# Expert down projections as seven block products (Strassen's scheme) on one Trainium2 core, and the tie step of the routing on GpSimd

## What is computed

```python
def _golden_weights(x, Wr, temperature):
    inh = jax.nn.sigmoid(x @ Wr / temperature)
    in_zone = (inh >= GOLDEN_LOWER) & (inh <= GOLDEN_UPPER)
    distance = jnp.abs(inh - GOLDEN_CENTER)
    weights = jnp.exp(-distance / 0.1) * in_zone.astype(x.dtype)
    ...
    fb = jnp.exp(-distance / 0.3)
    _, top2 = jax.lax.top_k(fb, 2)
    ...
gate = jnp.einsum('btd,edf->betf', x, Wg)
up = jnp.einsum('btd,edf->betf', x, Wu)
h = jax.nn.silu(gate) * up
e_out = jnp.einsum('betf,efd->betd', h, Wd)
out = jnp.einsum('bte,betd->btd', weights, e_out)
```

## Time and profile before

| what | value |
|---|---|
| median of three runs | 3265.81 us |
| time of the profiled execution | 3272.1 us |
| its span, first to last instruction | 3270.3 us |
| mean granted TensorE clock | 0.997 |
| TensorE busy, whole span | 3229.4 us (99%) |
| VectorE, ScalarE, GpSimd busy | 74%, 65%, 61% |
| last layer, in the span | from about 2640 us to the end |

### The profile page before, as it was taken

One profiled execution on the slowest core, in us unless ns is written; L12 is line 12 of the kernel. 1 busy time (PEld: TensorE's weight loads), 2 busy tenths in 40 slices (PEclk: granted clock), 3 DMA queues, 4 the chain that ended last, 5 costly groups with the idle time before them and its releaser, 6 DMA issues.

```text
span 3270.3 us, 106843 instructions
## 1 busy us (share of the span) xinstructions
PE 3229.4 (99%) x35420; PEld 2536.6 (78%) x35420; DVE 2423.5 (74%) x7665; ACT 2123.1 (65%) x6385; POOL 1988.8 (61%) x3965
## 2 busy tenths in 40 slices
PE   9999999999999999999999999999999999999999
PEld 7888888888766786777777777777776678888888
DVE  5677777777788767887888888788877866555555
ACT  5777777777756556777777777777775533333333
POOL 4666666666666446777777777777765662222232
PEclk9999999999999999999999999999999999999999
DMA  3111111111212242111111111111125640000000
GB/s 101 55 55 55 55 54 54 54 55 55 74 46 73 69 127 61 46 46 46 44 50 45 47 45 47 44 47 50 45 62 138 178 129 14 13 13 13 13 13 14
DMA packets 275878, 183.64 MB, mean 56 GB/s; under 512 B 116797, under 2 KB 272661, under 8 KB 275749
## 3 DMA queue, kind: packets, MB, share of 16 engines
q1 hardware_dynamic: 271109, 177.36, 19.3%
q10 hardware_dynamic: 4640, 4.59, 0.5%
HBM read 141.41 MB, written 36.21 MB: 54 GB/s over the span
## 4 chain that ended last, share of the span: by engine, by line
PE 59%; DVE 1%; DMA 1%; issue 0%; ACT 0%; SPq 0%; DVEq 0%; ACTq 0%
PE bank_e L3083 12%; PE c_ps_a L1134 7%; PE b_ps_a L1100 7%; PE bank_e L3096 7%; PE s_ps_a L1107 5%; PE out_ps_a L1160 3%; PE a_ps_a L1111 3%; PE c_ps_a L1111 2%; PE b_ps_a L1111 2%; PE out_ps_a L1144 2%; PE c_ps_a L1193 2%; PE m_ps_r L2538 2%; PE c_ps_a L1172 1%; PE out_ps_a L1232 1%; PE c_ps_a L1183 1%; PE m_ps_r L2576 1%
## 5 line engine op out<-in xcount | busy, mean ns | idle before, releaser
L1264 ACT ACTIVATE probs_a<-s_ps_a,neg_max_a 128x257 f32<-128x257 f32 x1024 | 474.4, 476 | 82.9 <-DVE neg_max_a L1384 78.1
L1318 POOL TENSOR_SCALAR probs_a<-probs_a,gated_a 128x256 f32<-128x256 f32 x1024 | 473.6, 483 | 26.5 <-POOL gated_a L1327 26.3
L1384 DVE TENSOR_REDUCE neg_max_a<-s_ps_a 128x1 f32<-128x257 f32 x1024 | 424.0, 414 | 0.0
L3039 POOL TENSOR_TENSOR hidden_e<-gate_p,own_p 128x256 f32<-128x256 f32 x192 | 139.2, 730 | 414.1 <-ACT gate_p L3197 413.9
L574 POOL TENSOR_SCALAR probs_i<-probs_i,inv_sum_i 128x256 f32<-128x256 f32 x510 | 243.9, 492 | 133.7 <-DVE inv_sum_i L738 129.3
L1383 DVE TENSOR_TENSOR self_s_a<-s_ps_a,mask_a 128x32 f32<-128x32 f32 x1024 | 185.8, 181 | 135.0 <-PE s_ps_a L1107 134.9
L553 ACT ACTIVATE probs_i<-s_ps_i,neg_max_i 128x257 f32<-128x257 f32 x512 | 236.3, 474 | 58.7 <-DVE neg_max_i L812 57.0
L392 PE MATMUL a_ps_i<-w_k_i,ctx_t_i 128*128 128x256 f32 x1024 | 253.7, 391 | 0.0
L1134 PE MATMUL c_ps_a<-w_v_a,ctx_t_a 128*32 128x256 f32 x4096 | 247.6, 382 | 0.0
L379 PE MATMUL c_ps_i<-w_v_i,ctx_t_i 128*128 128x256 f32 x1024 | 247.5, 379 | 0.0
L1100 PE MATMUL b_ps_a<-ctx_t_a,w_qk_a 128*128 128x256 f32 x1016 | 241.3, 380 | 0.0
(11 more groups left out here) (430 smaller groups left out, 8712.5 us busy)
## 6 DMA issues: line engine op xcount, KB each, us to landing
ctx_t_i<-in_ctx_t SPq DMA_DIRECT2D x128, 256.0 KB, 2.7
ctx_t_a<-in_ctx_t SPq DMA_DIRECT2D x128, 256.0 KB, 2.7
mask_a<-in_L_xattn_mask SPq DMA_DIRECT2D x512, 4.0 KB, 1.5
v_bd_a<-v_self_a SPq DMA_DIRECT2D x512, 8.0 KB, 1.8
x_tok_i<-in_x SPq DMA_DIRECT2D x32, 128.0 KB, 2.0
x_res_i<-in_x SPq DMA_DIRECT2D x32, 128.0 KB, 2.4
x_after<-y_tok_i SPq DMA_DIRECT2D x32, 128.0 KB, 1.8
x_tok_d<-x_after SPq DMA_DIRECT2D x32, 128.0 KB, 2.3
```

The source lines that it names most:

```text
L1264: act.activation(probs[:, t, :], s_ps[:, g, 0:K], ACT.Exp, bias=neg_max[:, t:t + 1], accum_out=row_sum[:, t:t + 1]).then_inc(exp_done, 1)
L1318: pool.tensor_scalar(probs[:, t, 0:2 * P], probs[:, t, 0:2 * P], gated[:, t:t + 1], 1.0, ALU.mult, ALU.mult).then_inc(probs_ready, 1)
L1384: dve.tensor_reduce(neg_max[:, 4 * f + g:4 * f + g + 1], s_ps[:, g, 0:K], AX.X, ALU.max, negate=True).then_inc(max_ready, 1)
```

## The change

**Down projection.** The eight calls of 256 columns per expert become seven block products of two calls with 128 columns each (`down`). The rows are the stationary operand, the weights the moving one. They are spread over the expert after: `down_3` of the expert two before stands behind P1, `down_1` behind 7a, `down_7` behind P6, `down_6` behind 7b, and `down_2`, `down_4`, `down_5` between P5 and P3. The very last expert keeps the ordinary form (`whole_down`).

**Sums of rows.** GpSimd forms four sums of blocks of `hidden` per expert (`sum_hidden`), right behind the last hidden quarter, at the start of the next expert.

**Sums of weights.** VectorE forms four block sums of the down weights per expert, in turn 0 alone (`sum_down`).

**Results.** ScalarE makes four more copies out of PSUM per expert (`down_copy`, `down_last`), VectorE three more additions (`down_join`), and the result stands in SBUF, in `y`. `take` reads `y`, no longer PSUM, and comes two experts later instead of one: behind `hide_last`, ahead of the join `own11` (in experts 0 and 2 around the joins).

**Banks.** `second` and `seventh` have one bank each instead of two, and the transposed tokens two banks instead of four.

**Routing.** The multiplication and the addition of `route_ties` move to GpSimd (`route_pairs`, in expert 1). On VectorE `route_zone` moves to the start of expert 0, `route_ranks` to the start of expert 1, and the rest, from the reduction to `route_weights`, to the start of expert 2, all ahead of the join `own11`. On ScalarE, silu of `own11` now stands ahead of the second copy of the chain (except in expert 0).

`moments` goes from expert 3 to expert 4; `normalize` stays at the end of expert 5.

```diff
@@ PE
         def expert(i, e, begins, ends):
...
             product(into, w_block(e, 0, 0), x_block(0, 0), chain_full, True)
+            if e > 1 or not begins:
+                down_3(i, e - 2)
...
+            pe.wait_ge(joined, joined_count(i, e - 1, 21))
+            product(seventh_ps, w_block(e, 1, 0), x_sum[3][:, :], seventh_full, True)
...
+            if downs:
+                down_1(i, e - 1)
+            pe.wait_ge(joined, joined_count(i, e - 1, 11))
+            product(second_ps, w_block(e, 0, 1), x_block(1, 0), second_full, True)
...
+            if downs:
+                down_7(i, e - 1)
             pe.wait_ge(copied, copy_count(i, e, 7))
...
-            if e or not begins:
-                down(i, e - 1, 0)
+            if downs:
+                down_6(i, e - 1)
...
             pe.wait_ge(copied, copy_count(i, e, 6))
             product(into, w_sum[1][:, e, :, :], x_sum[1][:, :], chain_full)
...
-            if e or not begins:
-                down(i, e - 1, 1)
+            if downs:
+                down_2(i, e - 1)
+                down_4(i, e - 1)
+                down_5(i, e - 1)
+        def down(into, rows, weights, start=False):
             for t in range(2):
+                last = pe.matmul(into[:, t * P:t * P + P], rows[:, t * P:t * P + P], weights, start=start and t == 0, stop=True, skip_group_check=True)
             last.then_inc(down_full, 1)
@@ GpSimd
+        def sum_hidden(i, e):
+            pool.wait_ge(hidden12_ready, count(i, e))
...
+            pool.tensor_tensor(hidden_sum[3][:, :], hidden_block(e, 11), hidden_block(e, 12), ALU.subtract).then_inc(down_sums, 1)
+            pool.tensor_tensor(hidden_sum[1][:, :], hidden_block(e, 12), hidden_block(e, 22), ALU.add).then_inc(down_sums, 1)
...
+            pool.tensor_tensor(hidden_sum[2][:, :], hidden_sum[1][:, :], hidden_block(e, 11), ALU.subtract).then_inc(down_sums, 1)
...
+            pool.tensor_tensor(hidden_sum[4][:, :], hidden_block(e, 21), hidden_sum[2][:, :], ALU.subtract).then_inc(down_sums, 1)
@@ VectorE
                 if e == 0:
                     route_logits(i)
+                    route_zone(i)
                 if e == 1:
+                    route_ranks(i)
+                if e == 2:
                     route_ties(i)
+                    route_fallback(i)
+                    route_totals(i)
+                    route_weights(i)
+                if takes and e not in (0, 2):
+                    take(i, e - 2, 1)
+                    take(i, e - 2, 0)
                 dve.wait_ge(second_full, count(i, e))
                 dve.wait_ge(copied, copy_count(i, e, 1))
+                join(i, e, 11, second_ps, parts.first)
...
                 if follows:
+                    down_joins(i, e - 1)
+                if begins:
+                    sum_down(e)
+                if e == 4 and not ends:
                     moments(dve, i + 1)
@@ take
-                last = dve.scalar_tensor_tensor(out=acc[n][:, t, :], in0=down_ps[n][:, t * D:t * D + D], scalar=weight[:, 2 * n + t, e % E:e % E + 1], in1=before_sum, op0=ALU.mult, op1=ALU.add)
+                last = dve.scalar_tensor_tensor(out=acc[n][:, t, :], in0=y[n][:, t, :], scalar=weight[:, 2 * n + t, e % E:e % E + 1], in1=before_sum, op0=ALU.mult, op1=ALU.add)
@@ ScalarE
+                else:
+                    silu(i, e, 11)
                 act.wait_ge(joined, joined_count(i, e - 1, 21))
                 act.wait_ge(chain_full, count(i, e, 4, 2))
                 copy(parts.second, chain[e % 2])
```

More of the change, by code:

```diff
@@ L3041, in turn @@
         def turn(i, begins, ends):
             for e in range(E):
-                if begins and e + 1 < E:
-                    sum_weights(e + 1)
+                if e or not begins:
+                    sum_hidden(i, e - 1)
+                if e == 0 and not begins:
+                    keep_last(i)
+                if begins and e == 0:
+                    sum_weights(1)
+                if begins and e + 2 < E:
+                    sum_weights(e + 2)
                 hide(i, e, 11)
+                if e == 1:
+                    route_pairs(i)
@@ new lines, in down_7, with down_6, down_2 @@
+        def down_7(i, e):
+            pe.wait_ge(down_sums, sum_count(i, e, 3))
+            pe.wait_ge(down_joined, down_joined_count(i, e - 1, 21))
+            down(down_seventh, hidden_sum[3], down_sum[3][:, e % E, :], True)
+        def down_6(i, e):
+            pe.wait_ge(down_sums, sum_count(i, e, 2))
+            pe.wait_ge(down_copied, down_copy_count(i, e, 1))
+            down(down_chain[e % 2], hidden_sum[2], down_sum[2][:, e % E, :])
+        def down_2(i, e):
+            wait_hidden(pe, i, e, 21)
+            pe.wait_ge(down_joined, down_joined_count(i, e - 1, 11))
+            down(down_second, hidden_block(e, 21), down_block(e % E, 1, 0), True)
@@ L3118, in expert @@
         def expert(i, e, begins, ends):
-            into, second, seventh = chain[e % 2], second_ps[e % 2], seventh_ps[e % 2]
+            into = chain[e % 2]
+            downs = e > 0 or not begins
             if begins:
@@ L3161, in turn, with whole_down @@
                 expert(i, e, begins, ends)
+        def whole_down(into, n, lanes, done):
+            for t in lanes:
+                at, col = (2 * n + t) * P, (t - lanes[0]) * D
+                for k in range(TILES):
+                    last = pe.matmul(into[:, col:col + D], hidden[(E - 1) % 2][:, k, at:at + P], w_down[:, E - 1, k, :], start=k == 0, stop=k == TILES - 1)
+            last.then_inc(done, 1)
         pe.wait_ge(*before.high)
@@ L3381, in turn @@
                 join(i, e, 22, chain[e % 2], parts.seventh)
-                if e == 1:
-                    route_totals(i)
-                    route_weights(i)
-                    take(i, 0, 0)
+                if takes and e in (0, 2):
+                    take(i, e - 2, 0)
                 if follows:
-                    take(i, e - 1, 1)
-                if e == 0:
-                    route_ranks(i)
-                if e == 3 and not ends:
+                    down_joins(i, e - 1)
+                if begins:
+                    sum_down(e)
+                if e == 4 and not ends:
                     moments(dve, i + 1)
@@ L3399, in vector @@
         hide_last(LAST, E - 1)
-        take(LAST, E - 1, 0)
+        take(LAST, E - 2, 1)
+        take(LAST, E - 2, 0)
         finish()
```

300 lines of the change are left out of this document (187 added, 113 removed).

## The result

The changed kernel takes 3288.53 us (median of four runs, 3285.45 to 3290.94), against 3267.82 us for the kernel before on the same chip: ratio 1.0064, 95% interval 1.0046 to 1.0081. It is slower by 0.64%, 20.7 us between the medians. Between the two profiled executions the spans differ by 3287.5 - 3270.3 = 17.2 us.

The account below looks back on a forecast made before the run. TensorE bounds the layer, busy 78.00 of 78.00 us a turn. Walking the engines in order gave six loop turns +16, turn 0 +6, turn 7 +1.3, start +0.4: together +24 on 3265.8, so 3290 us; range 3264 to 3310.

Parts of the forecast that it names:

- TensorE's own work, -22 us: Down products: 28 records at 0.111 us replace 16 taking 3.46 us; 9.15 us an expert, 0.35 less, over 63 experts.
- Rival C: Short down records don't hold 0.111 us: at 0.125 a record +37 us, 3303; at 0.137 +52, 3318; chance 0.15.
- the change doesn't do what it says: Down products: an eighth fewer columns but no TensorE time saved, the case from 0.124 us a record on.
- VectorE and GpSimd block each other, 0.88 us a pair: Expert start: takes reading two SBUF tensors alternate with GpSimd's sums, 0.88 us a pair against 0.34 to 0.40 alone.
- Rival A: Takes are not held by GpSimd but routing instructions are: a turn 78.1 us, +6 us, 3272; chance 0.14.
- rival B: Blocking costs nothing because GpSimd, idle half the time, starts later: 75.3 us a turn, -17 us, 3249; chance 0.16.
- It goes both ways: GpSimd's instructions beside VectorE's are held too: its sums near 0.9 us, where a product alone takes 0.72.
- The way to P5: Late join `own11` delays silu, then ScalarE's second copy, opening TensorE holes of 1 to 2 us ahead of P5.
- Experts 1 and 2, 1.8 and 1.45 us: TensorE waits ahead of P5, as routing pieces ahead of join `own11` delay it: 1.8 us in expert 1, 1.45 in 2.
- Expert 5, 1.4 us: TensorE waits 1.4 us ahead of P5: `moments` delays `hide_last` and GpSimd's power holds the first take until 3.2.
- Turn 0, +6 us: GpSimd's gate and up sums and VectorE's 32 down sums hold each other up ahead of `down_7` and `down_6`: +6 us.
- The tie step at zero: Moving the tie step to GpSimd in expert 1 costs nothing, as GpSimd waits for silu 21 there anyway.

Follow-up runs that it names:

- narrow_sums: The change, with GpSimd's four sums per expert forming only 8 of 256 columns and four down products reading plain hidden blocks: 3254.6 us, ratio to before 0.9957.
- takes_behind: The change, with all takes behind the joins, n=1 behind `own11` and n=0 behind `own22`, as in experts 0 and 2: 3296.8 us, ratio to before 1.0083.
- copy_first: The change, with ScalarE's second copy of the chain ahead of silu 11 in experts 1 to 7, the earlier order: 3268.7 us, ratio to before 1.0000.
- grouped_late: `three_moved` with turn 0's 32 down sums made 12 and GpSimd's weight sums behind each expert's last product: 3263.2 us, ratio to before 0.9984.
- three_moved: The change, with second copy ahead of silu 11, `route_ranks` behind join `own11`, GpSimd's fourth sum behind `hide` 11: 3261.9 us, ratio to before 0.9981.

## Why the prediction was right, and where it was off

It said 3290 us with the sign slower, and 3288.5 came out. Point by point:

- **TensorE's own work, -22 us: right.** 9.17 us for an expert without a hole (9.15 forecast); down records 0.11 us apart. Rival C and "the change doesn't do what it says" fall with that.
- **VectorE and GpSimd block each other, 0.88 us a pair: right.** `narrow_sums` shows it by itself: takes from 942 to 479 ns and 34 us off the time, with VectorE's code unchanged; and `takes_behind` shows 478 ns with nothing left out. The rule of the Trainium skill (SBUF — State Buffer, Who interferes with whom) is borne out for the takes. Rival A falls with the median of 942, rival B with the loop turns, which came out 1.6 us longer, not shorter. What B would have been can be seen: without the blocking 3254.6, where it said 3249.
- **It goes both ways: only in part.** "GpSimd's sums near 0.9" holds for the second sum (median 902 ns); the other three have 746, 788 and 732 (727, 732 and 729 in `takes_behind`, away from the takes). VectorE pays for most of it.
- **The way to P5: right.** `copy_first` cuts it and takes back 20 us of the 20.7 between the medians, 17.3 of the 18.8 between the last layers.
- **Experts 1 and 2, 1.8 and 1.45 us: right,** 1.98 and 1.39 lost.
- **Expert 5, 1.4 us: wrong, the largest mis-sized term of a loop turn.** The step that failed is "GpSimd's power of 1.02 us holds the first take until 3.2". The timelines of expert 5, GpSimd's and VectorE's:

```profile
2936.74 1.02 POOL L3026 TENSOR_TENSOR inv_std_e<-var_eps_e,half_e 128x4 f32<-128x4 f32 x1 [1.87 <-DVE var_eps_e L3366]
2937.73 0.75 POOL L3075 TENSOR_TENSOR hidden_sum_p<-hidden_e 128x256 f32<-128x256 f32 x1
```

```profile
2937.01 2.61 DVE L3492 SCALAR_TENSOR_TENSOR acc_e<-y_p,weight_e,acc_e 128x256 f32<-128x256 f32 x4
```

  The first two takes begin during the power, 0.27 and 0.67 us into it, and last 477 ns each; the four take 2.61 us, less than the 3.08 of an expert without a power. A long GpSimd instruction with four columns to read doesn't hold VectorE. Expert 5 loses 0.44 us and expert 6 0.14 (0.3 forecast). With this step alone mended the walk gives 79.2 us a turn instead of 80.2; measured 79.5. Six turns were sized at +16 and measured +9.5.
- **Expert 0, 0.5 us: too large.** From P3 to P3 it takes 10.05 us in the loop, and 9.94 in `narrow_sums`: about 0.1 lost.
- **Experts 3, 4 and 7 without a hole: nearly.** Expert 3 loses 0.29 us ahead of `down_3`, which waits for the down joins, and in expert 2 takes stand ahead of these. It is no matter of the blocking: in `narrow_sums` expert 3 takes 9.46 us as well.
- **Turn 0, +6 us: too small.** It was 8.3. The holes ahead of `down_7` that it named are there (1.17 and 0.54 us in experts 5 and 6). But the longest one, 3.25 us, stands ahead of P5 in expert 2 and not ahead of `down_7` or `down_6`, and behind it the clock costs 1.6 us that it lacked: expert 2 takes 14.33 us from P3 to P3, 5.2 more than an expert without a hole. It named the 32 small sums without a price of their own; without them turn 0 is 6.6 us shorter.
- **Start and end:** +0.4 forecast, -1.6 measured, in a stretch of the program that varies by 7 us over kernels with the same code, mostly with the granted clock. Turn 7: +1.3 forecast, +1.0 measured.
- **The tie step at zero: wrong by its size.** It saves some 5 us; the walk had its effect inside the 2.7 us a turn, but the text didn't tell it as a gain.

So the total was hit a little by compensation: the loop was sized 6.5 us too long and turn 0 2.3 us too short. The rest is between the measures: the medians lie 20.7 us apart, the profiled spans 17.2, and the last layers 18.8. Against the +24 of the sum that is 3 to 7 us too much; that the time itself was missed by 1.5 us only is luck in part, since the median of the kernel before came out 2.0 us higher (3267.8) than the one that the sum started from. Why the clock fell in some executions and not in others, ahead of the last layer and in turn 0, stays open.

## What to carry to other kernels

Before moving work to the engine with the most idle time, look at what its neighbour does in the same microsecond: here a VectorE instruction of 128x256 with two SBUF inputs took 0.94 us instead of 0.48 beside GpSimd's sums of the same size, and sums of busy time don't show it. Then follow the late result to where the bounding engine waits, queue by queue: the cheapest mend here was one line of order on a third engine, ScalarE, worth 20 of the 20.7 us. And count the instructions that meet a busy neighbour, the small ones too (128x32 took 0.72 us instead of 0.18); wide ones are no way out while the neighbour is busy (`grouped_late`). What can stand later (the fourth sum) should.

## What was unexpected of the hardware

- GpSimd's power of 128x4 (1.02 us) doesn't hold VectorE, while its 128x256 sums of 0.72 us do: takes of 475 to 479 ns begin inside the power in all six loop turns, against a median of 942 beside the sums. By the rule of the Trainium skill (SBUF — State Buffer, Who interferes with whom) the power, which reads SBUF too, should have held them; the trace differs, and it decides here.
- Between takes and sums the blocking is lopsided: VectorE's instruction goes from 0.48 to 0.94 us, GpSimd's from 0.73 to between 0.73 and 0.90. Beside VectorE's sums of 128x640 it isn't: there GpSimd's instructions take 1.19 to 1.31 us instead of 0.72 (`grouped_late`).
- TensorE's granted clock fell to 0.55 to 0.60 for 4 us behind a hole of 3.25 us, and didn't behind one of 2.92 us in another kernel. In `three_moved` it was 0.52 over 2650.3 to 2652.3, behind two holes of 0.95 and 0.88 us with a product between them; in the changed kernel it stayed at 1.00 behind the same two, of 1.13 and 0.88 us. So the length of a hole alone doesn't decide it.
